# A macaron block (FFN, attention, FFN) on one core: another opening for the first step, and routing tiles moved into PSUM

## The reference

```python
x = x + 0.5 * ffn(layernorm(x), ...)      # x: 4 x 1024 x 128, float32
x = x + attention(layernorm(x), ...)      # no softmax: 32 heads of 4, with a group norm
x = x + 0.5 * ffn(layernorm(x), ...)

def ffn(x):                               # rows of 128
    scores = sigmoid(x @ router_w.T)      # 16 experts
    s = scores + bias
    # 4 groups of 4 experts: a group's score is the sum of its two best;
    # the 2 best groups stay, of these the 4 best experts
    tw = scores of the 4 experts, divided by their sum, times 2.5
    h = silu(x @ gate_w[e]) * (x @ up_w[e]) @ down_w[e]      # all 16 experts
    routed = sum over e of combine[:, e] * h[e]
    return routed + silu(x @ sh_gate_w) * (x @ sh_up_w) @ sh_down_w   # 2 shared experts
```

## Time and profile before

| | us |
|---|---|
| median of 3 runs | 692.23 |
| lowest and highest | 690.93 and 693.77 |
| the profiled execution: time | 693.29 |
| its span in the profile | 691.6 |
| PE busy in the span | 661.9 (96%) |
| DVE, ACT, POOL busy | 535.9, 411.3, 442.0 |

### The profile page before, as it was taken

The page is one execution under the profiler, slowest core; times in us unless marked ns, Lnnn a source line. Parts: engine busy times, 40 slices in busy tenths (PEclk is TensorE's granted clock), DMA queues, the critical chain, the costliest instruction groups (busy, mean ns, idle before and its releaser), DMA issues.

```text
span 691.6 us, 11856 instructions
## 1 busy us (share of the span) xinstructions
PE 661.9 (96%) x3116; PEld 546.3 (79%) x3116; DVE 535.9 (77%) x1407; ACT 411.3 (59%) x820; POOL 442.0 (64%) x380
## 2 busy tenths in 40 slices
PE   4498999999999999999999999999999999999997
PEld 3386888888878888788887888878888888888885
DVE  4788796969788686986869868698686987969664
ACT  5465656565675655756557665575656565665553
POOL 5665666675775566756667566675567666665664
PEclk9699999999999999999999999999999999999999
DMA  7820614060603307033060330703306051240600
GB/s 219 285 92 2 245 64 181 4 244 0 245 1 105 142 2 245 0 102 143 0 245 0 108 137 16 245 0 122 138 16 245 16 181 65 103 159 20 241 15 16
DMA packets 30402, 76.31 MB, mean 110 GB/s; under 512 B 3585, under 2 KB 12305, under 8 KB 30353
## 3 DMA queue, kind: packets, MB, share of 16 engines
q1 hardware_dynamic: 30352, 75.79, 30.5%
HBM read 73.16 MB, written 2.62 MB: 110 GB/s over the span
## 4 chain that ended last, share of the span: by engine, by line
PE 85%; DVE 5%; issue 4%; SPq 3%; DMA 1%; ACT 1%; DVEq 0%; POOLq 0%; POOL 0%
PE gateP L417 9%; PE gateP L419 9%; PE gateP L418 9%; PE upP L417 9%; PE yP L417 9%; PE yP L419 9%; PE upP L419 8%; PE upP L418 8%; PE yP L418 8%; DVE T L958 2%; SPq L252 1%; PE prepP L448 1%; PE backP L433 1%; PE attP L463 1%; PE prepP L441 1%
## 5 line engine op out<-in xcount | busy, mean ns | idle before, releaser
L316 POOL TENSOR_TENSOR A_lo<-A,A_hi 128x512 fp32r<-128x512 f32 x288 | 371.6, 1292 | 208.7 <-ACT A_hi L711 208.0
L694 ACT ACTIVATE gateP<-gateP 128x512 f32<-128x512 f32 x256 | 148.8, 581 | 184.9 <-PE gateP L419 183.0
L958 DVE TENSOR_TENSOR T<-gateP,CB 128x512 f32<-128x512 f32 x256 | 175.1, 684 | 78.3 <-ACT gateP L694 71.0
L711 ACT CAST A_hi<-A 128x512 fp32r<-128x512 f32 x288 | 176.9, 614 | 46.7 <-DVE A L980 43.5
L980 DVE TENSOR_TENSOR A<-upP,T 128x512 f32<-128x512 f32 x256 | 177.0, 691 | 9.1
L417 PE MATMUL gateP<-XT_hi,W_hi 128*128 128x512 f32 x288 | 123.8, 430 | 9.1 <-DVE T L958 8.8
L417 PE MATMUL upP<-XT_hi,W_hi 128*128 128x512 f32 x288 | 114.2, 397 | 1.6 <-DVE A L980 1.6
L419 PE MATMUL gateP<-XT_lo,W_hi 128*128 128x512 f32 x288 | 113.9, 396 | 0.0
L418 PE MATMUL gateP<-XT_hi,W_lo 128*128 128x512 f32 x288 | 113.7, 395 | 0.0
L417 PE MATMUL yP<-A_hi,W_hi 128*128 128x512 f32 x288 | 113.1, 393 | 0.6 <-POOL A_lo L316 0.6
L419 PE MATMUL upP<-XT_lo,W_hi 128*128 128x512 f32 x288 | 113.2, 393 | 0.0
(11 more groups left out here) (159 smaller groups left out, 633.2 us busy)
## 6 DMA issues: line engine op xcount, KB each, us to landing
CB<-combT SPq DMA_DIRECT2D x128, 512.0 KB, 6.5
out_dram<-X SPq DMA_DIRECT2D x8, 256.0 KB, 2.0
X<-in_L_attn_x_dram SPq DMA_DIRECT2D x3, 512.0 KB, 6.1
W_in<-in_L_ffn_gate_w_dram SPq DMA_DIRECT2D x4, 256.0 KB, 5.3
W_in<-in_L_ffn_up_w_dram SPq DMA_DIRECT2D x4, 256.0 KB, 4.8
W_in<-in_L_ffn_down_w_dram SPq DMA_DIRECT2D x4, 256.0 KB, 5.6
X<-in_L_attn_x_dram SPq DMA_DIRECT2D x2, 256.0 KB, 4.4
combT<-CT SPq DMA_DIRECT2D x16, 32.0 KB, 1.8
```

The lines of the kernel that those rows point to most:

```text
L316: pool.tensor_tensor(A_lo[:, slot, :], A[:, slot, :], A_hi[:, slot, :].bitcast(F32), ALU.subtract).then_inc(low_done, 1)
L694: act.activation(dst, gateP[u % 2][:, :], ACT.Silu).then_inc(silu_done, 1)
L711: act.copy(A_hi[:, v % SLOTS, :], A[:, v % SLOTS, :]).then_inc(high_done, 1)
L958: dve.tensor_tensor(T[:, u % TS, :], gateP[u % 2][:, :], CB[:, e, :], ALU.mult).then_inc(gate_weighted, 1)
```

## The change

1. **DMA order.** x of block 1 is loaded before the shared weights; x of batches 2 and 3 and the small attention inputs after the `CB` loads of step 0.
2. **Spread on PE.** In step 0 the weights of the first four experts (units 2 to 5) don't go through DRAM: PE transposes one column of `comb`, broadcast to 128 columns, against the identity (`spread`, four matmuls of 128x128 for an expert) into `backP` or `attP`, and DVE takes them from there. For these units silu writes to `T` in SBUF. `CB` is loaded for the other 12.
3. **Order on PE.** Gate of units 0 to 3 and up of 0 and 1 come before the routing's result is waited for, 10 matmuls on a tile of ones fill in behind them, then the spread of two experts, `transpose_weights`, and up of 2 and 3. 15 such matmuls stand at PE's start. `transpose_weights` for step 1 moves to behind gate and up of unit 17; the transposes of the attention weights move from unit 6 to unit 20.
4. **Weight splits and statistics.** ACT makes `W_hi` in another order (units 0 and 1 ahead of the copy of `XT`); POOL splits units 2 and 3 in three pieces each and 4 to 9 one after each unit; DVE splits units 10 to 17 behind units 4 to 11 instead of 0 to 7. The statistics of block 1 run before step 0. ACT rounds `A` of units 0 and 1 behind unit 3, and of units 2 and 3 behind unit 4.
5. **Routing tiles in PSUM.** `rcl`, `score`, a second copy of `sel`, `eq`, `picked`, `wsel`, a second copy of the group scores and `grank` are columns 64 to 479 of `prepP`. Two instructions more make the copies; one `tensor_tensor` becomes a `tensor_reduce`. This holds in all 16 steps.

```diff
-                for g in range(E // CSEM):
+                for g in range(SPREAD // CSEM if first else 0, E // CSEM):
...
+            def spread(e):
+                for j in range(TILES):
+                    c = e * TILES + j
+                    mm = pe.transpose((backP, attP)[e % 2][:, j * P:(j + 1) * P],
+                                      comb[:, c:c + 1].broadcast_to([P, P]), ident[:, :])
+                mm.then_inc(spread_done, 1)
+            def keep_busy(count):
+                for _ in range(count):
+                    pe.matmul(yP[:, 0:P], ones[:, :], ones[:, :], start=True, stop=True)
+            def first_units():
+                for u in range(4):
+                    pe.wait_ge(w_lo_done, u + 1)
+                    if u == 0:
+                        pe.wait_ge(xt_lo_ready, 1)
+                    if u >= 2:
+                        pe.wait_ge(silu_done, u - 1)
+                    product(gateP[u % 2][:, :], W_hi[:, u, 0, :], W_lo[:, u, 0, :], XT_hi[:, 0, :],
+                            XT_lo[:, 0, :], True, True).then_inc(gate_done, 1)
+                    if u < 2:
+                        product(upP[u % 2][:, :], ...).then_inc(up_done, 1)
+                keep_busy(FILL)                       # FILL = 10
+                pe.wait_ge(route_seq, ROUTE_OPS)
+                spread(0)
+                spread(1)
+                transpose_weights(0)
+                for u in (2, 3):
+                    pe.wait_ge(mul_done, u - 1)
+                    product(upP[u % 2][:, :], ...).then_inc(up_done, 1)
...
+                for u in range(4 if first else 0, PAIR + (LAG if last else 0)):
+                    if first and SHARED + 2 <= u < SHARED + SPREAD:
+                        pe.wait_ge(gate_weighted, u - SHARED - 1)
+                        spread(u - SHARED)
...
+                    if first and u == UNITS - 1:
+                        transpose_weights(1)
...
             pe.wait_ge(const_seq, IDENT_AT)
+            keep_busy(WARM)                           # WARM = 15
...
+            def scratch(i, width=E):
+                at = TILES * (E * (i + 1))
+                return prepP[:, at:at + TILES * width].rearrange("p (t e) -> p t e", t=TILES)
+            rcl, score, selp, eqp, picked, wsel = (scratch(i) for i in range(6))
+            gscp = scratch(6, GROUPS)
+            grank = prepP[:, TILES * (7 * E + GROUPS):TILES * (7 * E + 2 * GROUPS)]
...
-                    dve.tensor_tensor(sel[:, :, :], score[:, :, :],
+                    for dst in (sel[:, :, :], selp):
+                        dve.tensor_tensor(dst, score, ...)
...
-                    dve.tensor_tensor(hi2[:, :, :], sel4[:, :, 0:2], sel4[:, :, 2:4],
+                    dve.tensor_tensor(hi2[:, :, :], sel4[:, :, 0:2], selp4[:, :, 2:4],
...
-                if e % CSEM == 0:
-                    dve.wait_ge(cb_in[e // CSEM], 16 * (t + 1))
-                dve.tensor_tensor(T[:, u % TS, :], gateP[u % 2][:, :], CB[:, e, :],
+                silu, weights = gateP[u % 2][:, :], CB[:, e, :]
+                if isinstance(t, int) and t == 0 and e < SPREAD:
+                    dve.wait_ge(spread_done, e + 1)
+                    silu, weights = T[:, u % TS, :], (backP, attP)[e % 2][:, :]
+                elif e % CSEM == 0:
+                    loads = t if e < SPREAD else t + 1
+                    dve.wait_ge(cb_in[e // CSEM], 16 * loads)
+                dve.tensor_tensor(T[:, u % TS, :], silu, weights,
...
-                    if first and u + AHEAD < UNITS:
-                        split_low(u + AHEAD)
+                    if first and 4 <= u and u - 4 + AHEAD < UNITS:
+                        split_low(u - 4 + AHEAD)
```

More of the change, by code:

```diff
@@ L129, in macaron_kernel @@
         left8 = sb("left8", [P, TILES, 8 - TOP_K + E])
-        wsel = sb("wsel", [P, TILES, E])
         wsum = sb("wsum", [P, TILES])
@@ L233, in gate_left @@
         def gate_left(step, w):
-            if w < SHARED:
+            if w < SHARED or (isinstance(step, int) and step == 0 and w < SHARED + SPREAD):
                 return silu_done, UNITS * step + w + 1
@@ L294, in _ @@
             spread_weights(0, True)
+            for b in range(2, BATCH):
+                sp.dma_start(X[:, b * BT:(b + 1) * BT, :], x_v[b]).then_inc(x_rest, 16)
+            for dst, src in small:
+                sp.dma_start(dst, src).then_inc(small_in, 16)
             with sp.Fori(1, NBLK + 1) as t:
@@ L566, in pair @@
                             logits(t0 + s + 1)
-                        if w == (16 if early else 11):
+                        if w == 11 and not early:
                             transpose_weights(t0 + s + 1)
@@ L691, in pair @@
                             dst = S[:, u % 2, :]
+                        elif first and u < SHARED + SPREAD:
+                            if u >= SHARED + 2:
+                                act.wait_ge(mul_done, u - 1)
+                            dst = T[:, u % TS, :]
                         else:
@@ L695, in pair @@
                     if first and u == 1:
-                        copy_weights(0)
-                    if first and u == 7:
+                        for unit in range(AHEAD - 4, AHEAD):
+                            split_high(unit)
+                    if first and u == 20:
                         act.wait_ge(setup_psum, 2)
@@ L702, in pair @@
                             act.copy(matrix[:, :], attP[:, i * P:(i + 1) * P]).then_inc(setup_sb, 1)
[L703 to L711 removed]
+                    if first and (u == 3 or 4 <= u and u - 2 + AHEAD < UNITS):
+                        split_high(AHEAD if u == 3 else u - 2 + AHEAD)
+                    if first and u in (3, 4):
+                        if u == 3:
+                            copy_weights(0)
+                        for v in (2 * u - 6, 2 * u - 5):
+                            round_high(n, v, False)
+                        if u == 3:
+                            split_high(AHEAD + 1)
+                    elif u <= PAIR and not (first and u < 5):
+                        round_high(n, u - 1, not (first and u - 1 < SLOTS))
                     early = first and s == 0
@@ L736, in _ @@
             act.copy(RT[:, :], attP[:, 3 * P:3 * P + E]).then_inc(setup_sb, 1)
+            for unit in range(SHARED):
+                split_high(unit)
             next_full(0)
             next_high(0, 0)
-            for unit in range(SHARED):
+            for unit in range(SHARED, 4):
                 split_high(unit)
             route_silu(0)
-            for unit in range(SHARED, AHEAD):
+            for unit in range(4, AHEAD - 4):
                 split_high(unit)
@@ L831, in route @@
+                    eq = eqp.rearrange("p t (g h) -> p t g h", h=GROUPS)
                     dve.tensor_tensor(ahead[:, :, :, 0, :], other, own, ALU.is_gt).then_inc(route_seq, 1)
-                    dve.tensor_tensor(eq[:, :, :, :], other, own, ALU.is_equal).then_inc(route_seq, 1)
-                    dve.wait_ge(route_seq, base + 11)
-                    dve.tensor_tensor(ahead[:, :, :, 1, :], eq[:, :, :, :], before[:, :, :, :],
+                    dve.tensor_tensor(eq, other, own, ALU.is_equal).then_inc(route_seq, 1)
@@ L1013, in _ @@
             stats(0)
+            dve.wait_ge(x_second, 16)
+            rows(1, 1)
+            dve.wait_ge(rstd_ready, 2)
+            stats(1)
             dve.wait_ge(xt_hi_ready, 1)
@@ L1022, in _ @@
                 if part in (5, 6):
-                    dve.wait_ge(route_seq, 16 if part == 5 else 17)
+                    dve.wait_ge(route_seq, 18 if part == 5 else 19)
                 route(0, part)
```

163 lines of the change are left out of this document (82 added, 81 removed).

## The result

The changed kernel takes 681.31 us (median of four runs, 680.66 to 682.24) against 692.04 us before (690.93 to 693.77). The ratio is 0.985, with an interval of 0.983 to 0.987: faster by 10.7 us, where 9.9 was forecast (682.3).

What follows compares the result with a forecast made beforehand. PE, busy 661.9 of 691.6 us, bounds the kernel; only its idle time, slow clock or own work can give. Terms: -10.0 - 2.9 + 0.45 + 2.5 = -9.9 us, so 682.3 against the median, range 680 to 685.5 (chance 0.68).

Steps and rivals of the forecast that it cites:

- The start: Kernel start to the routing: fillers raise PE's clock, so near starts 1.0 us earlier, at 11.4; bounds 0 and 1.4.
- The routing of step 0: DVE, step 0: sel and hi lose 1.4 us of stalls, two instructions add 0.4; comb ready 6.9 us after near starts.
- The gap before unit 4: PE in step 0: weights avoid the store and load, so gate 4 starts at 21.2 instead of 31.16, -10.0 us.
- The clock at units 4 and 5: PE, unit 4 to the transposes: 18 matmuls at the upper clock take 4.1 us instead of 7.0, -2.9 us.
- DVE from unit 4 to 17: Later splits delay step 1's comb; PE loses 5.2 us where it lost 2.7: +2.5 us, bounds +0.5 and +5.
- Steps 1 to 15: Later routings on DVE lose stalls and gain two instructions each; taken as 0, bounds -2 and +1 us.
- Rival A: DVE holds the first step more, 3.3 us a unit in units 4 to 11: 686 us; chance 0.15.
- B: PE's clock stays low at the start despite fillers, spread reached at 24.6 instead of 18.3 (+5.3): 688 us; chance 0.06.
- C: The attention loop's waits for T go too, up to 4.3 us, if routing parts cause them: 679 us; chance 0.07.
- D: PSUM operands cost DVE more in 16 routings; slower than before from 0.1 us an instruction, 699 at 0.12; chance 0.04.

Runs made afterwards that it cites:

- no_warm: The changed kernel without the 15 fillers at the head of PE; 683.18 us.
- no_psum: The changed kernel with the routing's tiles back in SBUF (20 instructions); 686.47 us.
- psum_only: The kernel before with the routing's tiles in PSUM and nothing else of the change; 689.01 us.
- no_spread: The changed kernel without the spreading on PE, all 16 experts' weights of step 0 going through DRAM; 688.51 us.
- sp_order2: The kernel before with sp_order's DMA order and the attention weights' transposes moved from unit 6 to unit 20; 688.85 us.
- both_new: The changed kernel with POOL, not DVE, splitting the weights of units 14 to 17, and ACT copying step 1's CT ahead of the rounding of A; 678.52 us.
- pool_split: The changed kernel with only the splits of units 14 to 17 moved to POOL, CT copied where the change has it; 679.46 us.
- best: both_new without the ten fillers behind the gate of unit 3; 677.24 us.
- best_gaps: best with three fillers behind the first transposes and two behind the logits; 677.66 us.
- sp_order: The kernel before with SP's loads of x of batches 1 to 3 and ten small inputs issued after step 0's CB loads; 696.8 us.

## Why the prediction was right

It was right in the result and in its two large terms, and partly by parts that offset one another. The sum was made against the profiled execution, and there it gave 9.9 us where the traces differ by 12.6; the medians, 10.7 us apart, are nearer to it because the profiled execution of before was slow for its kernel and that of after fast. The 2.7 us are, by the stretches above: 0.5 in the start of unit 4, 0.6 in units 8 to 17, 1.3 from step 1 on, less 0.15 at units 4 and 5, and 0.4 between units 6 and 8, for which there was no term (0.25 of it is the attention weights' transposes, which come back at unit 20).

- **The start.** `near` at 11.08 instead of 12.40, -1.3 where -1.0 was taken. no_warm shows the two slow groups back, with `near` at 12.38, and costs 0.8 to 1.9 us.
- **The routing of step 0.** 6.7 us, 6.9 predicted. `sel` and `hi` are never over 0.23. Of the 1.1 us by which it is shorter than before, the tiles make 0.7: in no_psum it takes 7.4. The stalls of `sel` and `hi` there are 0.39 and 0.35, where the kernel before has 0.92 and 0.90, so the rest came with the other edits, which no run separates. psum_only shows the tiles alone: 1.3 us less wait at the first `comb`, hidden there behind the DMAs, and 1.8 at the second.
- **The gap before unit 4.** Unit 4 at 20.64 (21.2 predicted), -10.5 where -10.0 stood. no_spread gives 7.3 us of it back in its trace, of which 2.8 are the low clock and the fillers and some 4.5 the way over memory. The rest is the shorter routing and the order on SP: sp_order2 alone moves the same point by 3.15. These parts don't add up to one sum. With the spread most of the order's gain should be superfluous there, since the weights that come by DMA are needed later; the changed kernel with the old order was not run.
- **The clock at units 4 and 5.** 20.64 to 25.34 is 4.70 us with a spread of four transposes in it (0.36 to the next gate), where it took 7.0. Predicted were -2.9 for the clock and +0.45 for the spread, so -2.45; measured is -2.3.
- **DVE from unit 4 to 17.** +2.5 predicted, +1.9 measured from unit 8 to step 1. This is the term that was out in its parts. `comb` came 23.5 us after the gate of unit 8 and not 25.1: T of unit 8 stood 2.0 us behind its gate instead of 2.6, and from there to the end of `comb` it was 21.5 us instead of 22.5. The four splits in it (0.61, 1.06, 0.54 and 1.67) make 3.9 us, not far from the 3.6 taken. What was priced too low is the stalls that go, 1.2 us: in the kernel before they make 2.1 in this stretch, and 0.9 of that is a `tensor_scalar` of 128x4 with one input, which took 1.06; the prediction let it stay, and it takes 0.19 now. The waits in units 8 to 17 were to make 5 us; by `comb` PE has lost 3.6 (23.5 against the 19.9 of the forecast). Against that, 1.15 of the loss is a wait that the prediction didn't have: with `transpose_weights(1)` right before the transposes of the next input, these need `CT` copied out of the shared `prepP`, and ACT rounds A of a unit first. both_new removes it, and pool_split, which doesn't, keeps it.
- **Steps 1 to 15.** 0 predicted, -1.3 measured, 1.0 of it in the loop's four waits (4.3 to 3.3). The PSUM tiles are not needed for it: no_spread, which has them, has 3.2 there, but no_psum 3.0 and sp_order2 3.5 without any. All thirteen other traces lie between 3.0 and 3.7; the 4.3 stands in the one trace of the kernel before, so it may be that execution as well as that program. Why it differs stays open.
- **Rival A** (DVE holds the first step) was right in kind and less in size; **B** (a low clock at the start) had something in it that was put wrongly: the fillers do bring the clock up, but it falls again at 11 us in some executions, at a price of 1.5 us in the trace and not 5.3 (which by the rival's own times, 24.6 and 18.3, should read 6.3). **C** has one microsecond of its 4.3, and not by its cause. **D**, a price for PSUM operands, is excluded: 223 against 225 ns for the same instruction, the same `sel` took 225 with both inputs in SBUF (median in the kernel before), and psum_only is faster. Only the reciprocal is 8 ns longer, 561 against 553, with its output in PSUM. The rule of the Trainium skill ("VectorE: DVE Perf Modes", section on the TRN2 errata), by which an instruction that reads PSUM costs more, is not borne out by these rows either.

The mechanism for the stalls, two inputs in SBUF beside a busy POOL, was argued from rows in the prediction. psum_only and no_psum now show the effect in both directions: the longest `comb` is 1379 and 1373 ns with both inputs in SBUF, 276 and 277 with one in PSUM. One of the long ones in the kernel before starts at 553.83 us and takes 1.37, beside POOL's `A_lo`, which runs from 553.78 for 1.29. The Trainium skill, in "SBUF — State Buffer", section "SBUF: two separate sides", says that a DVE operation with two SBUF inputs and a GpSimd operation that reads SBUF lock one port pair against each other; the traces agree with it for `comb`. They also hold a stall of an instruction with a single input: the `tensor_scalar` on `wsum`, in SBUF in all kernels, took up to 1.06 us before and 1.07 in no_psum, but 0.18 and 0.19 in psum_only and the changed kernel. Why moving other tiles frees it is not shown.

## What to carry to other kernels

A value that a later engine needs soon need not take the way over memory: four groups of four transposes, under half a microsecond each on the busiest engine, took a store and a load of 7.3 us off the path, because only the first four experts needed it. When a queue's order is changed, look first for who waits for what is now late: the same order on SP was 4.7 us slower with the transposes at unit 6 and 3.3 us faster with them at unit 20. Fillers belong where nothing useful can be behind them; ten ahead of a wait that had become short cost 1.5 us where the clock had fallen, and an idle time of 2.19 us in their place cost nothing.

## What was unexpected of the hardware

- The granted clock at 10 to 16 us differs between executions of one kernel: 1.00 in the first trace of the changed kernel, with 0.64 and 0.80 us of idle time ahead of transposes and logits, and down to 0.50 in the second, on the same instructions, with 1.51 and 0.80. But both_new and best fell too with no idle time ahead of the transposes. Of the nine traces with the head's fillers six have the fall and three don't.
- At the start of the kernel before and of no_warm the matmuls of the first units are 0.43 us apart, the spacing of the lower level, while the windows from 12 to 16 us show a granted clock of 1.00. There only the spacing tells the speed.
- After an idle time of 2.68 us PE kept the upper clock in the kernel before, and after 2.19 us in best_gaps; after 2.72 us in sp_order2 it fell to the lower level (1.2 GHz) for some 3 us, and in no_psum after 1.42 and 1.15 us close together.
- The store of 32 KB landed in 1.9 us in the changed kernel and in sp_order, where it stands alone, and in 3.3 and 3.55 us in psum_only and the kernel before, with the small inputs and loads ahead of it.
- DVE's splits of 128x384 took from 0.54 to 1.67 us in one step, with POOL busy beside them; POOL does the same split in 1.02 us.
